# Layer 1's product of u and D moved from ScalarE to VectorE in a four-layer megakernel

## The chip, the cores and the metric

The kernel runs on one core of one Trainium2 chip. The metric is the device time of one execution in microseconds (us), of which the median of several runs is given; less is better. TensorE (PE), VectorE (DVE), ScalarE (ACT), GpSimd (POOL) and SyncE (SP, which issues DMAs) each run a program of their own, strictly in order, and wait for one another by semaphores.

## What is computed

Sixteen sequences (B = 16) of 256 tokens and 256 channels pass through four layers: two state-space layers (layer 0 with two scans in opposite directions, layer 1 a Mamba block), then two attention layers. All is float32. The part that matters here is in layer 1:

```python
xm = silu(conv(x @ W_in))                 # u: 256 tokens x 512 channels
dt = softplus(dtr @ W_dt + b_dt)
def step(hst, inp):                       # 16 states per channel
    hst = hst * exp(dt_t * A) + (dt_t * x_t) * B_t
    y = einsum('bds,bs->bd', hst, C_t)
y = ys + xm * D_param                     # "u times D"
y = y * silu(z)
```

So u is used twice: in the product of dt and u, which feeds the scan, and in u times D, which is added to the scan's output y. D holds one number per channel.

## The kernel before, in words

**Units and ticks.** All three state-space scans (s = 0 and 1 of layer 0, s = 2 of layer 1) are cut into units of one state and one half of the channels (256 channels on 128 partitions as two blocks, times 256 tokens: tiles of 128x512). There are 96 units per sequence (64 of layer 0 for sequence i, 32 of layer 1 for sequence i-1), 1,536 in all. A unit costs: `dbut`, two products of dt*u with B (one by ACT, L788, one by POOL, L798); four transposes by PE into `ps_b` (L710); `decay`, two exponentials by ACT (L777); the scan by DVE (L818, `hst`); `g`, the product with C by POOL (L833); and four transposes by PE that add g up in `ps_v` (L738). A unit u's scan waits for its transposed dbut and its decay; buffers are two to four units deep. PE transposes unit t+2 ahead of the work of tick t and adds up unit t-2 after it; ACT makes decays two units ahead.

**What lies between the units.** Everything else (norms, projections, the preparation of a scan, attention) is cut into pieces by Python generators, each `yield` a seam. Tables written by hand (`PLACES` for the usual sequence, `SPECIAL` for i = -1, 0, 1, 14 to 18) give for each stage and engine the tick at which each piece is put into that engine's program, behind that tick's unit work. Two pieces with the same tick stand in the order of the list `STAGES`. Nothing is decided at run time.

**The stage that the change touches** is `prep2`, the preparation of layer 1's scan, run once per sequence in the middle of layer 0's units of the next one:

- ACT (`prep_scalar`, L984): copies of projections, exp and log for delta (L1014, L1017); then, after DVE's product of delta and u, u times D in place, four instructions of 128x256 (L1022, each with D's column as the scale), with one seam behind the second; then two copies `dut` (L1029) of the transposed product, each after four transposes by PE (L978).
- DVE (`prep_vector`, L1031): two corrections of delta (L1037), the product delta*u into `du` (L1049, in the trace `pT`, since it shares that buffer; for the last sequence `dut`), a small memset of delta (L1051).
- PE (`prep_tensor`, L940): projections (L946, L968), transposes of `du` (L978); its last piece waits for both `dut` copies.

The semaphore `ud_done_2` tells that u times D is there. Only PE waits for it, when it begins to sum layer 1's first unit of that sequence and adds u in by transposes (L719); in the usual sequence that is at tick 66, whereas u times D has its place at tick 44.

**Around it, in the usual sequence** (ticks from the sequence's start): at tick 44 ACT has a table load and the silu of layer 2's tail (L874, `xt_x`), then both pieces of u times D, then the first `dut`; at tick 45 the second `dut`, which is preceded by another table load (L868, for the decays' exponential). PE at tick 44 has the output projection of layer 2 (L923, L927, which wait for `xt_x`) and the second set of transposes of du, and at tick 46 the first projection of `prep0` (L946) behind the wait for the second `dut`. DVE has the first half of layer 0's gating (L1221, `yg`) at tick 45 and at tick 46 the residual of layer 2 (L1594, which waits for PE's L927) with two rounds of norm statistics (L879, L882); from tick 48 on the scaling of the normed rows (L903, `yv`, `xn_l`). PE then transposes those (L910).

Of the kernel before, what the change touches and what calls it, by code (L numbers as in the profile page):

```python
# [10 lines left out]
ALU = mybir.AluOpType  # L11
ACT = mybir.ActivationFunctionType
# [5 lines left out]
TB, DB, EB = T // P, D // P, E // P  # L18
# [29 lines left out]
               dp0=EB, dp1=EB, dp2=EB, alog0=EB * N, alog1=EB * N, alog2=EB * N,  # L48
# [22 lines left out]
def offsets(widths):  # L71
    at, out = 0, {}
    for name, w in widths.items():
# [66 lines left out]
    },  # L140
    "prep2": {
        "PE": (30.875, 34, 35, 36, 39, 43, 44, 46),
        "ACT": (34, 36, 36.125, 39, 41, 41, 44, 44, 44, 45),
        "DVE": (40, 42, 43),
        "SP": (50, 120),
    },
    "l2a": {
# [120 lines left out]
        },  # L268
        "prep2": {
            "PE": (33, 33, 35, 36, 37, 41, 43, 44),  # L270
            "ACT": (33, 34, 36, 36, 36.667, 37, 41, 41, 41, 43),
            "DVE": (38, 39, 40),
            "SP": (35, 37),
        },
        "ada": {
# [41 lines left out]
        },  # L317
        "prep2": {
            "PE": (28, 31, 32, 34, 38, 43, 45, 46),
            "ACT": (32, 32, 37, 37, 40, 41, 44, 44, 44, 45),  # L320
            "DVE": (38, 42, 44),
            "SP": (46, 128),
        },
        "l2a": {
# [45 lines left out]
        },  # L370
        "prep2": {
            "PE": (21, 21, 22, 24, 28, 29.2, 29.8, 33.875),
            "ACT": (22, 23, 26, 26, 28.5, 28.75, 31.2, 31.4, 31.8, 32.4),
            "DVE": (27.25, 28.5, 29),
            "SP": (23, 25),
        },
        "l2a": {
# [41 lines left out]
        },  # L419
        "prep2": {  # L420
            "PE": (-10.444, -10.333, -10, -9.667, -7, -3, -1, -1),
            "ACT": (-7, -7, -6.5, -6.25, -4, -4, -1, -1, -1, -1),
            "DVE": (-7, -4, -3),
            "SP": (-9, -9),
        },
        "l2a": {
# [85 lines left out]
def build(nc, dram, out):  # L512
    with ExitStack() as ctx:
        def sb(name, shape, dt=F32):
            return ctx.enter_context(nc.sbuf_tensor(name, shape, dt))
# [4 lines left out]
        S = {n: ctx.enter_context(nc.semaphore(n)) for n in SEMS}  # L520
# [14 lines left out]
        c = {k: CO[:, o:o + n] for k, (o, n) in COFF.items()}  # L535
# [24 lines left out]
        def bank(ps_, k, m=None):  # L560
            return ps_[:, k, :] if m is None else ps_[:, k, :].rearrange("p (a n) -> p a n", a=m)
# [18 lines left out]
        u_s = [sb(f"u{s}", [P, EB, T]) for s in range(3)]  # L580
# [19 lines left out]
        def nth(sem, b, value):  # L600

            return b * EACH.get(sem, 1) + value

        def slot(b, s):

            if s == 0 and b == 0:
                return 2
            return 0 if s == 2 and b == LAST - 1 else s

        def du_of(b, s):  # L610

            if s == 2 and b == LAST - 1:
                return dut[1][:, :, :].rearrange("p t (h n) -> p (t h) n", n=T)
            return du
# [9 lines left out]
        def after(eng, b, sem, value):  # L624

            if 0 <= b < LAST:
                eng.wait_ge(S[sem], nth(sem, b, value))
# [237 lines left out]
        def logexp():  # L865

            if table[0] != TABLES:
                nc.scalar.preload_act_table_set(TABLES)  # L868
                table[0] = TABLES
# [114 lines left out]
        def prep_scalar(act, b, s, v, at):  # L984
            bk, i = bank(ps_v, v), slot(b, s)
            ch = act_chain[0]
            yield next(at)
            act.wait_ge(S[f"dbc_full_{s}"], nth(f"dbc_full_{s}", b, 1))
            if s == 0:
                after(act, b - 1, "dt_full_1", 2)  # L990
                after(act, b - 1, "c_stored_1", 16)
            if s == 2 and b < LAST - 1:
                after(act, b - 3, "y3_full", 1)
            elif s == 2:
                after(act, b, "dt_full_1", 2)
                after(act, b, "c_stored_1", 16)
            if s == 1 and b >= 1:
                after(act, b, "dt_full_0", 2)
                after(act, b, "c_stored_0", 16)
            if s == 2 and b == 0:  # L1000
                after(act, b, "dt_full_0", 2)
                after(act, b, "c_stored_0", 16)
            nc.scalar.activation(dbc[i][:, :], bk[0:DBC, 0:T], ACT.Identity,
                                 bias=dbcb[:, s:s + 1]).then_inc(S[f"dbc_sb_{s}"], 1)
            yield next(at)
            act.wait_ge(S[f"bt_full_{s}"], nth(f"bt_full_{s}", b, 1))
            nc.scalar.activation(bcm[i][:, :, :], bk[:, 0:TB * P].rearrange("p (t q) -> p t q", t=TB)[:, :, BROW:DBC],
                                 ACT.Copy).then_inc(S[f"bcm_sb_{s}"], 1)
            for k in range(2):
                yield next(at)  # L1010
                act.wait_ge(S[f"dt_full_{s}"], nth(f"dt_full_{s}", b, k + 1))
                d = delta[i][:, 2 * k:2 * k + 2, :]
                logexp()
                ch.done(nc.scalar.activation(d, bank(ps_v, v, 2), ACT.Exp))  # L1014
                yield next(at)
                logexp()
                nc.scalar.activation(d, d, ACT.Ln, bias=1.0).then_inc(S[f"sp_log_{s}"], 1)  # L1017
            yield next(at)
            act.wait_ge(S[f"du_ready_{s}"], nth(f"du_ready_{s}", b, 1))
            dp = (c["dp0"], c["dp1"], c["dp2"])[s]  # L1020
            for eb in range(EB):
                last = nc.scalar.activation(u_s[i][:, eb, :], u_s[i][:, eb, :], ACT.Copy, scale=dp[:, eb:eb + 1])  # L1022
                if eb == 1:
                    yield next(at)
            last.then_inc(S[f"ud_done_{s}"], 1)
            for t in range(TB):
                yield next(at)
                act.wait_ge(S[f"dut_full_{s}"], nth(f"dut_full_{s}", b, t + 1))
                nc.scalar.activation(dut[i][:, t, :], bk, ACT.Copy).then_inc(S[f"dut_sb_{s}"], 1)  # L1029

        def prep_vector(dve, ch, b, s, v, edge, at):  # L1031
            i, du = slot(b, s), du_of(b, s)
            for k in range(2):
                yield next(at)
                dve.wait_ge(S[f"sp_log_{s}"], nth(f"sp_log_{s}", b, k + 1))
                d = delta[i][:, 2 * k:2 * k + 2, :]
                nc.vector.scalar_tensor_tensor(out=d, in0=d, scalar=LN_TOP, in1=bank(ps_v, v, 2), op0=ALU.min,  # L1037
                                               op1=ALU.max).then_inc(S[f"dt_read_{s}"], 1)
            yield next(at)
            dve.wait_ge(S[f"dt_read_{s}"], nth(f"dt_read_{s}", b, 2))  # L1040
            if s == 2:
                after(dve, b + 1, "dut_full_1", 2)
                if b < LAST - 1:
                    after(dve, b - 2, "o_full_2", H2 // 2)
            elif s == 0:
                after(dve, b - 2, "dut_full_2", 2)
            else:
                after(dve, b, "dut_full_0", 2)
            nc.vector.tensor_tensor(du, delta[i][:, :, :], u_s[i][:, :, :], ALU.mult).then_inc(S[f"du_ready_{s}"], 1)  # L1049
            dve.wait_ge(S[f"du_ready_{s}"], nth(f"du_ready_{s}", b, 1))  # L1050
            ch.done(nc.vector.memset(delta[i][:, :, edge:edge + 1], RESET))  # L1051
            nc.vector.engine_nop().then_inc(S[f"prep_done_{s}"], 1)

        def prep_sync(sp, b, scans, s, at):
            yield next(at)
            sp.wait_ge(S[f"dbc_sb_{s}"], nth(f"dbc_sb_{s}", b, 1))
            scans.wait_c(sp)
            sp.dma_start(c_rows[slot(b, s)], dbc[slot(b, s)][CROW:CROW + N, :]).then_inc(S[f"c_stored_{s}"], 16)
            yield next(at)
            sp.wait_ge(S[f"c_stored_{s}"], nth(f"c_stored_{s}", b, 16))  # L1060
# [688 lines left out]
        with ExitStack() as pro:  # L1749
            stage_sems, S = S, {**dict(zip(FIRST, S.values())), **{k: S[k] for k in CARRIED}}  # L1750
# [270 lines left out]
        S = stage_sems  # L2021
# [54 lines left out]
        last = [(LAST - 1, s, hh) for s, hh in LAYER1]  # L2076
# [181 lines left out]
```

## Time and profile before

| | us |
|---|---|
| median of 3 runs | 3290.21 (3288.32 to 3298.6) |
| the profiled execution | 3297.11 |
| its span in the profile | 3295.4 |
| lies around the span | 1.7 |

| engine | busy us | share | instructions |
|---|---|---|---|
| PE | 3022.8 | 92% | 21772 |
| DVE | 2678.8 | 81% | 3433 |
| ACT | 2818.3 | 86% | 6502 |
| POOL | 2655.1 | 81% | 3086 |

The profile comes from one execution. "Busy" is the time in which at least one instruction of the engine runs; instructions overlap at their ends by some 0.1 us, so a row that merges two of 0.50 us shows 0.90. In a row, `out<-in` are the program's buffer names, `x4` is the number of instructions merged, and a bracket at the end gives the idle time of the engine before the row and what ended it. The granted TensorE clock has a mean of 0.98 of full speed.

### The profile page before, as it was taken

The page shows a single profiled execution, that of the slowest core. Times are in us where ns is not written, and L with a number is a line of the kernel's source. Part 1 is how long each engine was busy: PE and PEld are TensorE (multiplying, and loading weights), DVE is VectorE, ACT ScalarE, POOL GpSimd, SP SyncE. Part 2 cuts the span into 40 slices and gives each one's busy share as a digit, 9 for nine tenths or more (in the row PEclk, how much of TensorE's full clock was granted, in tenths as well). Part 3 has the DMA queues.
Part 4 walks back from the last instruction along what each step waited for, and adds up shares of the span by engine and source line. Part 5 has one row for each costly group of instructions (what it writes and reads, how often), then busy time and mean ns, then how long its engine had stood idle before and what let it go on. Part 6 is the DMA issues. An engine that isn't in the chain of part 4 may idle for free.

```text
span 3295.4 us, 63649 instructions
## 1 busy us (share of the span) xinstructions
PE 3022.8 (92%) x21772; PEld 2525.4 (77%) x21772; DVE 2678.8 (81%) x3433; ACT 2818.3 (86%) x6502; POOL 2655.1 (81%) x3086
## 2 busy tenths in 40 slices
PE   6778789999999999999999999999999999988896
PEld 3667677778787888888788887878788887876764
DVE  1667788979798988979898998979798997968762
ACT  2768878899999999999999999998999989887843
POOL 0787999889898898988898898989898897868730
PEclk8899999999999999999999999999999999999998
DMA  5121222222222222222222221222222222212100
GB/s 201 55 76 53 73 79 72 78 67 83 69 81 73 71 84 65 85 67 84 67 81 73 68 86 65 85 67 85 67 74 81 68 82 60 72 52 68 57 25 9
DMA packets 133872, 239.57 MB, mean 73 GB/s; under 512 B 15374, under 2 KB 31054, under 8 KB 133296
## 3 DMA queue, kind: packets, MB, share of 16 engines
q1 hardware_dynamic: 133552, 235.50, 23.3%
q8 instruction: 177, 2.90, 0.4%
q14 instruction: 143, 1.17, 0.1%
HBM read 230.36 MB, written 5.08 MB: 71 GB/s over the span
## 4 chain that ended last, share of the span: by engine, by line
PE 55%; ACT 21%; DVE 10%; POOL 7%; issue 5%; DVEq 0%; POOLq 0%; ACTq 0%
PE ps_b L710 12%; PE ps_v L738 12%; ACT decay L777 8%; DVE hst L818 5%; POOL g L833 5%; PE ps_v L917 5%; ACT dbut L788 4%; PE ps_x L923 3%; PE ps_x L1449 3%; PE ps_x L1476 3%; PE ps_v L968 3%; PE ps_v L923 2%; PE ps_x L917 2%; POOL dbut L798 2%; ACT L874 2%
## 5 line engine op out<-in xcount | busy, mean ns | idle before, releaser
L833 POOL TENSOR_TENSOR g<-hst,c_bc 128x512 f32<-128x512 f32 x1536 | 1975.6, 1286 | 428.4 <-PE ps_v L738 394.1
L818 DVE TENSOR_TENSOR_SCAN hst<-decay,ps_b 128x512 f32<-128x512 f32 x1536 | 1821.5, 1209 | 317.1 <-PE ps_b L710 170.6
L777 ACT ACTIVATE decay<-delta,acoef 128x256 f32<-128x256 f32 x3072 | 1379.2, 499 | 26.8 <-DVE hst L818 25.9
L710 PE MATMUL ps_b<-ident,dbut 128*128 128x128 f32 x6144 | 943.0, 277 | 150.2 <-DVE hst L818 65.9
L738 PE MATMUL ps_v<-ident,g 128*128 128x128 f32 x6144 | 941.7, 276 | 13.9 <-ACT u L1130 12.1
L710 PEld LDWEIGHTS ps_b<-ident,dbut 128*128 128x128 f32 x6144 | 706.9, 142 | 231.1 <-issue 138.8
L738 PEld LDWEIGHTS ps_v<-ident,g 128*128 128x128 f32 x6144 | 727.5, 142 | 143.9 <-issue 67.8
L798 POOL TENSOR_SCALAR dbut<-dut,bcm 128x256 f32<-128x256 f32 x1536 | 750.2, 489 | 79.9 <-ACT dut L1029 79.9
L788 ACT ACTIVATE dbut<-dut,bcm 128x256 f32<-128x256 f32 x1536 | 767.9, 501 | 31.5 <-PE ps_b L710 28.9
L1561 DVE TENSOR_REDUCE mxt<-ps_x 128x4 f32<-128x1024 f32 x120 | 144.6, 1205 | 10.1 <-PE ps_x L1449 10.1
L1532 ACT ACTIVATE pT<-ps_x 128x1024 f32<-128x1024 f32 x120 | 121.8, 1015 | 30.3 <-PE ps_x L1487 25.7
L1476 PE MATMUL ps_x<-qT,kT 32*128 32x256 f32 x960 | 135.9, 400 | 4.8 <-ACT pT L1532 4.5
L1449 PE MATMUL ps_x<-kT,qT 32*128 32x256 f32 x960 | 137.8, 404 | 0.0
L923 PE MATMUL ps_v<-weights,yg 128*128 128x256 f32 x512 | 128.1, 385 | 0.0
L917 PE MATMUL ps_v<-xt_a,weights 128*128 128x256 f32 x512 | 126.8, 382 | 0.1
L765 ACT ACTIVATE yt<-ps_v 128x512 f32<-128x512 f32 x64 | 38.0, 594 | 91.6 <-PE ps_v L738 91.6
L923 PE MATMUL ps_x<-weights,xt_l 128*128 128x256 f32 x384 | 106.7, 403 | 5.6 <-DVE kmax L1714 1.8
L1476 PEld LDWEIGHTS ps_x<-qT,kT 32*128 32x128 f32 x960 | 82.0, 184 | 34.9 <-issue 20.4
L1449 PEld LDWEIGHTS ps_x<-kT,qT 32*128 32x128 f32 x960 | 82.9, 186 | 26.1 <-issue 18.3
L923 PEld LDWEIGHTS ps_v<-weights,yg 128*128 128x128 f32 x512 | 91.1, 192 | 12.7 <-DVE yg L1221 2.6
L917 PEld LDWEIGHTS ps_v<-xt_a,weights 128*128 128x128 f32 x512 | 91.2, 192 | 10.0 <-DVE yg L1257 0.8
L1022 ACT ACTIVATE u<-u,columns 128x256 f32<-128x256 f32 x192 | 84.1, 499 | 6.8 <-DVE pT L1049 5.1
(264 smaller groups left out, 3614.9 us busy)
## 6 DMA issues: line engine op xcount, KB each, us to landing
c_bc<-c_rows SPq DMA_DIRECT2D x768, 256.0 KB, 3.1
weights<-in_weights_dram SPq DMA_DIRECT2D x1, 4320.0 KB, 24.3
x<-in_x_dram SPq DMA_DIRECT2D x16, 256.0 KB, 4.0
rows_bc<-mod_rows SPq DMA_DIRECT2D x16, 256.0 KB, 3.9
gate<-mod_rows SPq DMA_DIRECT2D x32, 128.0 KB, 3.6
out_dram<-x SPq DMA_DIRECT2D x16, 256.0 KB, 3.5
wc<-in_wc_dram SPq DMA_DIRECT2D x1, 2048.0 KB, 11.2
maskrow<-mask_rows SPq DMA_DIRECT2D x16, 128.0 KB, 3.3
```

Of the source, the lines that this page charges most:

```text
L710: last = nc.tensor.matmul(ps_b[:, u % 2, e * T + t * P:e * T + (t + 1) * P], dbut[:, u % NDBU, t, e * P:(e + 1) * P], ident[:, :], is_tran ...
L738: last = nc.tensor.matmul(ps_y[:, t, e * P:(e + 1) * P], g[:, u % NG, e, t * P:(t + 1) * P], ident[:, :], is_transpose=True, start=False, ...
L777: last = nc.scalar.activation(decay[:, u % (DA_AHEAD + 2), e, :], delta[slot(b, s)][:, eb, :], ACT.Exp, scale=acoef[:, s, eb, n:n + 1])
L788: nc.scalar.activation(dbut[:, u % NDBU, 0, :], dut[k][:, 0, hh * HALF * P:(hh + 1) * HALF * P], ACT.Copy, scale=bcm[k][:, 0, n:n + 1]).th ...
L798: nc.gpsimd.tensor_scalar(dbut[:, u % NDBU, 1, :], dut[k][:, 1, hh * HALF * P:(hh + 1) * HALF * P], bcm[k][:, 1, n:n + 1], 1.0, ALU.mult, ...
L818: nc.vector.tensor_tensor_scan(line(hst[:, u % NHST, :, :].rearrange("p e t -> p (e t)")), line(decay[:, u % (DA_AHEAD + 2), :, :].rearran ...
L833: nc.gpsimd.tensor_tensor(g[:, u % NG, :, :], hst[:, u % NHST, :, :], c_bc[:, k % NCB * CHUNK + n % CHUNK, :].unsqueeze(1) .broadcast_to([ ...
L917: last = nc.tensor.matmul(dst, weight[:, k, m0:m0 + m], rhs[:, k, :], start=(k == 0), stop=(k == kb - 1))
L923: last = nc.tensor.matmul(dst, lhs[:, k, t * P:(t + 1) * P], weight[:, k, :], start=(k == 0), stop=(k == kb - 1))
L1449: last = nc.tensor.matmul(bank(pair, j, TB)[:, q, :], a.q[r:r + LANE, hb, q * P:(q + 1) * P], a.k[r:r + LANE, hb, :], start=True, stop=True)
L1476: last = nc.tensor.matmul(bank(pair, j % 2, 2)[:, j // 2, :], a.k[r:r + LANE, hb, m * P:(m + 1) * P], a.q[r:r + LANE, hb, :], start=True, ...
L1561: nc.vector.tensor_reduce(by_head[:, 2 * g_:2 * g_ + 2, :, KEY_AT[g_ // 2 % 2] + 1], a.pairs[g_ % len(a.pairs)][:, 0:2, :].rearrange("p j ...
```

## The change

For s = 2 alone, the four ACT instructions of u times D are left out. DVE makes them instead, as `tensor_scalar` with a multiply by D's column, in two pieces of two instructions, placed one and two ticks behind its product of delta and u (in the usual sequence ticks 44 and 45). `ud_done_2` is now incremented by DVE. All other places stay as they were: ACT's list loses the two entries of u times D, DVE's gains two. At equal ticks `prep2` stands before `l0_post` in `STAGES`, so that the second piece comes before `yg` at tick 45.

```diff
@@ PLACES (usual sequence)
     "prep2": {
         "PE": (30.875, 34, 35, 36, 39, 43, 44, 46),
-        "ACT": (34, 36, 36.125, 39, 41, 41, 44, 44, 44, 45),
-        "DVE": (40, 42, 43),
+        "ACT": (34, 36, 36.125, 39, 41, 41, 44, 45),
+        "DVE": (40, 42, 43, 44, 45),
@@ SPECIAL, i = 1
-            "ACT": (33, 34, 36, 36, 36.667, 37, 41, 41, 41, 43),
-            "DVE": (38, 39, 40),
+            "ACT": (33, 34, 36, 36, 36.667, 37, 41, 43),
+            "DVE": (38, 39, 40, 41, 42),
@@ i = 14
-            "ACT": (32, 32, 37, 37, 40, 41, 44, 44, 44, 45),
-            "DVE": (38, 42, 44),
+            "ACT": (32, 32, 37, 37, 40, 41, 44, 45),
+            "DVE": (38, 42, 44, 45, 46),
@@ i = 15
-            "ACT": (22, 23, 26, 26, 28.5, 28.75, 31.2, 31.4, 31.8, 32.4),
-            "DVE": (27.25, 28.5, 29),
+            "ACT": (22, 23, 26, 26, 28.5, 28.75, 31.8, 32.4),
+            "DVE": (27.25, 28.5, 29, 30, 31),
@@ i = 16
-            "ACT": (-7, -7, -6.5, -6.25, -4, -4, -1, -1, -1, -1),
-            "DVE": (-7, -4, -3),
+            "ACT": (-7, -7, -6.5, -6.25, -4, -4, -1, -1),
+            "DVE": (-7, -4, -3, -2, -1),
@@ prep_scalar
-            yield next(at)
-            act.wait_ge(S[f"du_ready_{s}"], nth(f"du_ready_{s}", b, 1))
-            dp = (c["dp0"], c["dp1"], c["dp2"])[s]
-            for eb in range(EB):
-                last = nc.scalar.activation(u_s[i][:, eb, :], u_s[i][:, eb, :], ACT.Copy, scale=dp[:, eb:eb + 1])
-                if eb == 1:
-                    yield next(at)
-            last.then_inc(S[f"ud_done_{s}"], 1)
+            if s < 2:
+                yield next(at)
+                act.wait_ge(S[f"du_ready_{s}"], nth(f"du_ready_{s}", b, 1))
+                dp = (c["dp0"], c["dp1"])[s]
+                for eb in range(EB):
+                    last = nc.scalar.activation(u_s[i][:, eb, :], u_s[i][:, eb, :], ACT.Copy, scale=dp[:, eb:eb + 1])
+                    if eb == 1:
+                        yield next(at)
+                last.then_inc(S[f"ud_done_{s}"], 1)
@@ prep_vector
             nc.vector.engine_nop().then_inc(S[f"prep_done_{s}"], 1)
+            if s == 2:
+                for pair in range(2):
+                    yield next(at)
+                    for eb in (2 * pair, 2 * pair + 1):
+                        last = nc.vector.tensor_scalar(u_s[i][:, eb, :], u_s[i][:, eb, :], c["dp2"][:, eb:eb + 1], None,
+                                                       ALU.mult)
+                last.then_inc(S["ud_done_2"], 1)
```

## Rows read from the trace of the kernel before

**Rows 1.** The page, busy time and share of the span of each engine.

```profile
PE 3022.8 (92%) x21772; PEld 2525.4 (77%) x21772; DVE 2678.8 (81%) x3433; ACT 2818.3 (86%) x6502; POOL 2655.1 (81%) x3086
```

**Rows 2.** ACT's groups of instructions: busy us, mean ns | idle before, releaser.

```profile
L1022 ACT ACTIVATE u<-u,columns 128x256 f32<-128x256 f32 x192 | 84.1, 499 | 6.8 <-DVE pT L1049 5.1 <-DVE dut L1049 1.7
```

**Rows 3.** The chain of waits, 1629 to 1643 us: start, us, what.

```profile
1632.69 1.59 ACT u L1022 x4
```

**Rows 4.** ACT in order of time, 1627 to 1641 us.

```profile
1630.37 1.28 ACT L874 ACT_TABLE_LOAD   x1
1631.67 1.02 ACT L874 ACTIVATE xt_x<-ps_x,mod_cols 128x256 f32<-128x256 f32 x2
1632.58 1.70 ACT L1022 ACTIVATE u<-u,columns 128x256 f32<-128x256 f32 x4
...
1637.28 0.58 ACT L1029 ACTIVATE dut<-ps_v 128x512 f32<-128x512 f32 x1
```

**Rows 5.** PE in order of time, 1630 to 1643 us.

```profile
1632.74 1.13 PE L923 MATMUL ps_x<-weights,xt_x 128*128 128x256 f32 x4 [0.61 <-ACT xt_x L874]
...
1637.91 1.12 PE L946 MATMUL ps_v<-xt_b,dbcw 128*112 128x256 f32 x4 [0.55 <-ACT dut L1029]
...
1639.36 0.63 PE L710 MATMUL ps_b<-ident,dbut 128*128 128x128 f32 x4
...
1641.59 0.66 PE L910 MATMUL ps_x<-ident,yv 128*128 128x128 f32 x4 [0.30 <-DVE yv L903]
```

**Rows 6.** DVE in order of time, 1628 to 1642 us.

```profile
1630.14 2.33 DVE L818 TENSOR_TENSOR_SCAN hst<-decay,ps_b 128x512 f32<-128x512 f32 x2
...
1632.97 1.21 DVE L818 TENSOR_TENSOR_SCAN hst<-decay,ps_b 128x512 f32<-128x512 f32 x1
1635.21 0.69 DVE L1594 TENSOR_TENSOR x<-ps_x,x 128x512 f32<-128x512 f32 x1 [1.03 <-PE ps_x L927]
...
1638.02 2.34 DVE L818 TENSOR_TENSOR_SCAN hst<-decay,ps_b 128x512 f32<-128x512 f32 x2
1640.28 1.26 DVE L903 TENSOR_SCALAR yv<-x,mv,nrm 128x256 f32<-128x256 f32 x2
```

**Rows 7.** DVE's L1594 in the first and the last of 11 equal sequences.

```profile
698.77 0.69 DVE L1594 TENSOR_TENSOR x<-ps_x,x 128x512 f32<-128x512 f32 x1 [1.03 <-PE ps_x L927]
...
2570.80 0.69 DVE L1594 TENSOR_TENSOR x<-ps_x,x 128x512 f32<-128x512 f32 x1 [1.03 <-PE ps_x L927]
```

**Rows 8.** Busy us (and instructions) of PE, PEld, DVE, ACT, POOL; clock, DMA.

```profile
1641.50:1672.50 31.00, 30.89 (x220) 27.39 (x221) 27.66 (x32) 29.94 (x75) 28.19 (x33) 1.00 0.23 72
```

**Rows 9.** DVE's nearest instructions by their line: ns min/median/max, first and last start.

```profile
L1999 DVE TENSOR_SCALAR gather<-itok,token x2: 346/350/353, 47.1 to 47.3; 128x256 f32<-128x256 f32 x2
...
L903 DVE TENSOR_SCALAR yv<-yv,mv,nrm x2: 391/398/406, 1628.0 to 1628.3; 128x256 f32<-128x256 f32 x2
...
L903 DVE TENSOR_SCALAR xn_a<-x,mv,nrm x2: 1446/1936/2425, 1550.6 to 1552.9; 128x256 f32<-128x256 f32 x2
```

**Rows 10.** POOL in order of time, 1628 to 1643 us.

```profile
1630.98 0.48 POOL L798 TENSOR_SCALAR dbut<-dut,bcm 128x256 f32<-128x256 f32 x1
1631.63 1.27 POOL L833 TENSOR_TENSOR g<-hst,c_bc 128x512 f32<-128x512 f32 x1 [0.16 <-PE ps_v L738]
1632.87 0.48 POOL L798 TENSOR_SCALAR dbut<-dut,bcm 128x256 f32<-128x256 f32 x1
1636.20 1.27 POOL L833 TENSOR_TENSOR g<-hst,c_bc 128x512 f32<-128x512 f32 x1 [2.85 <-PE ps_v L738]
```

**Rows 11.** PE in sequence i = 2, and DVE near the end of the steady part.

```profile
509.57 0.65 PE L978 MATMUL ps_v<-ident,pT 128*128 128x128 f32 x4 [1.62 <-ACT dut L1029]
...
3095.85 0.61 DVE L1728 SCALAR_TENSOR_TENSOR shared<-ps_x,kmax,blockmask 128x128 f32<-128x128 f32 x2 [0.51 <-PE ps_x L1652]
```

## The prediction

> **What bounds the kernel now.** I read the page first: PE is busy for 92% of the span, the others for 81 to 86% [rows 1]. That says PE leads on average, not that it leads where the change is. So next I took ACT's groups: u times D is 192 instructions and 84.1 us of ACT [rows 2]; a third of it, 64 instructions of layer 1, moves. 84.1 / 3 = 28 us of ACT's busy time go. Then the chain of waits in one usual sequence: it does contain the four instructions, 1.59 us of them [rows 3]. Taken literally that promises 1.6 us per sequence. The rest of this prediction is about why I don't take it.
>
> Next came the engines in order of time over the same stretch. The reader is to follow two strands that both begin with ACT's silu `xt_x`, which stands ahead of u times D.
>
> Strand one (ACT): table load from 1630.37, silu to 1632.69, u times D from 1632.58 for 1.70, and at its end the second `dut` at 1637.28 [rows 4]. PE waits 0.55 us for that `dut` and starts L946 at 1637.91 [rows 5].
>
> Strand two (PE and DVE): PE starts layer 2's output projection at 1632.74, as soon as the silu is there [rows 5]; DVE's residual L1594 waits for its end and starts at 1635.21, after 1.03 us idle; behind it come the norm statistics, and only at 1638.02 the next scans [rows 6]. PE's transposes for the scan two units on start at 1639.36, and they need the scan that began at 1638.02 and, by the row's mean, took 1.2 us [rows 5, 6]. DVE goes on without a break to `yv` at 1640.28, and PE waits 0.30 us for that at 1641.59 [rows 5, 6]. From there PE is full: 30.89 of 31.00 us [rows 8].
>
> So both strands end at PE, and strand two ends last: when PE has been let go early at 1637.91, it stops again at 1639.36 for the scan. Nothing of strand two passes through u times D. And what moves PE's start at 1641.59 moves the whole sequence, for in the 31 us behind it there is no idle time in which to catch up [rows 8]. DVE's idle 1.03 us before L1594 is all the slack that strand two has; it is the same in the first and the last of 11 sequences (i = 3 to 13) [rows 7].
>
> **The change part by part.**
>
> *ACT loses four instructions per sequence.* 1.70 us of ACT go [rows 4], 1.6 of them net. The first `dut` comes 1.6 us earlier, but PE reaches the transposes behind it only after the projection, so nobody gains. The second `dut` comes about 1.5 us earlier and PE's 0.55 us at 1637.91 vanish [rows 5]. PE does its L946 and one sum of states, and then waits for the scan at 1639.36 as it did. Gain at the end of the stretch: 0. What hides the gain is DVE's work from 1635.21 to 1639.2; if that were gone, up to 1.6 us per sequence would show.
>
> *DVE gains four instructions per sequence,* two behind the scan that starts at 1630.14 and two behind the next, before `yg` and before the scan of 1632.97 [rows 6]. All four lie ahead of L1594. The trace has none of this form from DVE. The nearest rows: `gather`, also 128x256 from SBUF to SBUF with one column as scalar, 350 ns, two of them starting 0.2 to 0.3 us apart; `yv<-yv`, with two columns, about 400 ns, starts 0.3 apart, both pairs while POOL does nothing long [rows 9]. That is the lower bound, 0.3 us each. The upper one is `xn_a`, of the same shape as the latter: 1.45 and 2.43 us in one sequence [rows 9], with nothing different but what POOL is doing; 1.9 us each. Between them stands `yv<-x` at 1640.28, 1.26 us for two, 0.63 each [rows 6]. A gain from the added work is excluded, since nothing waits for it before tick 66.
>
> Which it is follows from POOL's rows. A pair that meets a POOL instruction is longer by about what is left of it. The first pair would start at about 1631.3: POOL's `dbut` ends at 1631.46, its next `g` starts at 1631.63 [rows 10]; the pair fits between if it is let in first: 0.6 us. This puts the scan and the second pair to about 1633.0: `g` ends at 1632.90 or a little later and a `dbut` of 0.48 stands behind it, after which POOL is idle until 1636.20 [rows 10]. So the second pair costs 0.6 plus a piece of a dbut: 0.75 us. Sum 1.35 us, against 4 x 0.3 = 1.2 as the lower end. The upper end, with `g` (1.27) let in before the second instruction and a whole dbut before the third and the fourth, is 1.2 + 1.27 + 2 x 0.48 = 3.4 us. I take 1.35 because the stretch is nearer to `gather` and `yv<-yv`: POOL is idle for 2.85 us of it.
>
> Per sequence: 1.35 - 1.03 = 0.32 us later. `yg` and the scan of 1632.97 are late by up to 1.35 too, but PE asks for them only after 1636 (it is in the projection from 1632.74 on), so that is covered.
>
> Here the Trainium skill speaks against the change. Its page "SBUF — State Buffer", section "Who interferes with whom", says that VectorE and GpSimd share one pair of ports, which a `tensor_scalar` in a two-port mode holds alone for the whole instruction, whoever comes second waiting in full. The 1.45 and 2.43 us of `xn_a` beside the 0.35 of `gather` agree. By that rule alone, with a wait at each of the four, the sum would be the upper end, 3.4 us.
>
> *The other five sequences.* i = 1: ACT waits for PE before `dut` anyway and DVE idles soon after; 0. i = 2: PE waits 1.62 us for the first `dut` [rows 11], the one place where u times D is plainly in the way; but the scans behind it come later by the 1.35, so of 1.6 gained I count 0 and keep -1 to +0.5 for the range. i = 14 and 15: DVE idles for microseconds there; 0. i = 16: the first pair comes before L1728, which has 0.51 us idle before it [rows 11], in a stretch where POOL has two `g` back to back; +0.5, at most +1.5.
>
> *The sum.* 11 x 0.32 + 0.5 = 3.5 + 0.5 = 4.0 us. The profiled execution took 3297.1, so 3301.1 of its kind; that execution lies 6.9 above the median of the three runs, and the sum is a difference, so I put it on the median: 3290.2 + 4.0 = 3294. No DMA is issued or moved and no queue of SP or POOL is passed. DVE has no new wait.
>
> **The rivals.**
>
> 1. *POOL wins the race (slower).* In the first pair, the second instruction asks at about 1631.6, when `g` at 1631.63 is just about to start [rows 10]. If `g` comes first, the pair costs 0.6 + 1.3 and the second then meets an idle POOL: 0.6. That is 2.5 us, 2.5 - 1.03 = 1.5 us per sequence, 11 x 1.5 + 0.5 = 17, giving 3307. If it only half meets it, 1.0 per sequence, 3302. It decides from 0.85 us per sequence on ((9.9 - 0.5) / 11, the 9.9 being the 0.3% below). For it: `xn_a` [rows 9], and that all 11 sequences are alike, so that a lost race is lost 11 times. Against: `g` waits for PE until 1631.6, after the pair has begun. Chance 0.26. (The Trainium skill, "SBUF — State Buffer", "Who interferes with whom", says that the first to start keeps the pair of ports; it does not say who is first here.)
> 2. *The chain of waits is right (faster).* ACT's strand is the longer one: then 1.6 us per sequence less, in 13 sequences 20.8 us, or, cut by DVE's 0.32, 1.3 x 11 = 14: 3270 to 3276. For it: the chain [rows 3], and ACT shows no idle time from 1629 to 1641. Against: DVE's rows, which are as unbroken and hold L1594, whose releaser is PE. Chance 0.09.
> 3. *All is covered (no change).* The pairs cost 1.2 or less and the two ends cancel; 3290. It differs from my forecast in a size that can't be measured and shares its chance, 0.65 together.
>
> **How the numbers follow.** A measurement of this kernel tells some 0.3% from no change, 9.9 us here (the three runs lie 10 us apart). Forecast and rival 3 (3287 to 3298): within, 0.65. Rival 1: mostly slower, a little of it still within; I give 0.24 to slower and 0.02 to within. Rival 2: 0.09 to faster. That makes 0.09, 0.67 and 0.24. The range is to leave out 0.2: 0.09 for rival 2 and the rest above the upper end. Low end: no cost and a gain of 1 at i = 2, less what runs scatter, 3285. High end: rival 1 at 1.5 per sequence and +1.5 at i = 16, 3290.2 + 16.5 + 1.5 = 3308.
>
> **What would show it.** In the changed profile: the ACT group u<-u has 128 instructions and the new DVE group 64, with a mean of 350 to 450 ns if I am right, above 700 if rival 1 is. DVE's idle time before L1594 falls from 1.03 to about 0, and L1594 is late. PE's 0.55 us before L946 is gone, and PE stands instead at the L710 after it, released by DVE's scan. The distance between two sequences grows from 187.2 us ((2570.80 - 698.77) / 10, [rows 7]) by 0.3. If it shrinks by more than 0.9, my reading of strand two is wrong; if the new instructions cost over 0.6 us each, the price is.

## The result, and the profile after

The changed kernel took 3300.78 us (median of 9 runs, 3295.16 to 3305.24) against 3290.21 of the kernel before (9 runs beside it): a ratio of 1.0029, 95% interval 1.0019 to 1.0038. That is 6 to 13 us slower, about 10, just at the 0.3% that were named as the bound of what can be told. A second set of the same kernel gave 3299.38 and 1.0026 (1.0013 to 1.0039). The forecast was 3294.0, range 3285 to 3308. So the range held the time, but 10 is not 4, and the steps have to be looked at one by one. The profiled execution after took 3303.45 us, its span 3301.7. Medians and ratios, here and below, leave out one slow execution in each of two variants (14402 and 3872 us).

The page after, busy time and share of each engine, to be read against [rows 1]:

```profile
PE 3022.4 (92%) x21772; PEld 2526.3 (77%) x21772; DVE 2705.4 (82%) x3497; ACT 2794.5 (85%) x6438; POOL 2658.8 (81%) x3086
```

DVE has 64 instructions more and ACT 64 fewer. ACT's busy time falls by 23.8 us (28 had been put down), DVE's grows by 26.6. PE's busy time is the same to 0.4 us, so what the change costs is, by this profile, idle time of PE. By the new code's lines (ns: minimum, median, maximum; then the first and the last start), the moved work:

```profile
L1058 DVE TENSOR_SCALAR u<-u,columns x64: 321/336/1401, 319.3 to 3106.9; 128x256 f32<-128x256 f32 x64
```

Median 336 ns, but a maximum of 1401: most of the 64 went undisturbed, some did not. Which ones matters. First the usual sequence, the counterpart of [rows 6]; DVE in order of time:

```profile
1633.96 0.59 DVE L1058 TENSOR_SCALAR u<-u,columns 128x256 f32<-128x256 f32 x2
1634.46 1.21 DVE L818 TENSOR_TENSOR_SCAN hst<-decay,ps_b 128x512 f32<-128x512 f32 x1
1635.60 0.59 DVE L1058 TENSOR_SCALAR u<-u,columns 128x256 f32<-128x256 f32 x2
1636.10 0.68 DVE L1229 TENSOR_TENSOR yg<-ps_v,act_x 128x512 f32<-128x512 f32 x1
1636.70 1.21 DVE L818 TENSOR_TENSOR_SCAN hst<-decay,ps_b 128x512 f32<-128x512 f32 x1
1637.89 0.69 DVE L1602 TENSOR_TENSOR x<-ps_x,x 128x512 f32<-128x512 f32 x1
...
1640.70 2.30 DVE L818 TENSOR_TENSOR_SCAN hst<-decay,ps_b 128x512 f32<-128x512 f32 x2
1642.92 1.28 DVE L903 TENSOR_SCALAR yv<-x,mv,nrm 128x256 f32<-128x256 f32 x2
```

Each pair puts off what stands behind it by 0.50 us (1633.96 to 1634.46; 1635.60 to 1636.10), 1.0 in sum. The residual, L1594 before and L1602 now, had 1.03 us of idle time before it [rows 6] and now has no bracket. From it to `yv` there are 5.03 us, before 5.07. The slack was used up almost exactly, and nothing was carried on. PE over the same stretch, the counterpart of [rows 5]:

```profile
1635.42 1.13 PE L923 MATMUL ps_x<-weights,xt_x 128*128 128x256 f32 x4 [0.60 <-ACT xt_x L874]
...
1639.87 1.03 PE L946 MATMUL ps_v<-xt_b,dbcw 128*112 128x256 f32 x4
...
1642.04 0.63 PE L710 MATMUL ps_b<-ident,dbut 128*128 128x128 f32 x4 [0.70 <-DVE hst L818]
...
1644.25 0.66 PE L910 MATMUL ps_x<-ident,yv 128*128 128x128 f32 x4 [0.28 <-DVE yv L903]
```

The 0.55 us before L946 are gone, and 0.70 us before the next L710 have appeared, released by DVE's scan: a wait for ACT was exchanged for a wait for DVE. From the projection's start to the transposes of `yv` it is 8.83 us now, 8.85 before (1632.74 to 1641.59). And over ten sequences DVE's rows, to be read against [rows 7]:

```profile
701.32 0.69 DVE L1602 TENSOR_TENSOR x<-ps_x,x 128x512 f32<-128x512 f32 x1
...
2573.05 0.69 DVE L1602 TENSOR_TENSOR x<-ps_x,x 128x512 f32<-128x512 f32 x1
```

(2573.05 - 701.32) / 10 = 187.17 us per sequence; before 187.20. **The 11 usual sequences cost nothing.** So the 6 to 13 us lie outside them. At i = 1 one sees the other kind of instruction. DVE:

```profile
319.29 1.60 DVE L1058 TENSOR_SCALAR u<-u,columns 128x256 f32<-128x256 f32 x2
320.82 1.21 DVE L818 TENSOR_TENSOR_SCAN hst<-decay,ps_b 128x512 f32<-128x512 f32 x1
321.95 1.64 DVE L1058 TENSOR_SCALAR u<-u,columns 128x256 f32<-128x256 f32 x2
```

and POOL at the same time:

```profile
319.46 1.28 POOL L833 TENSOR_TENSOR g<-hst,c_bc 128x512 f32<-128x512 f32 x1
...
322.16 1.27 POOL L833 TENSOR_TENSOR g<-hst,c_bc 128x512 f32<-128x512 f32 x1 [0.93 <-DVE hst L818]
```

A pair takes 1.60 and 1.64 us instead of 0.59, and in each pair it is the second instruction (at 319.53 and 322.19) that takes 1.4: it asks 0.07 and 0.03 us after POOL's `g` has started, and is done only 0.15 us after that `g`. The first ones take 0.3. In the usual sequence it is the other way round: the second instruction starts at 1634.21, and `g` at 1634.31. That is rival 1, but not in the eleven sequences in which it was feared: twice in i = 1, and once each in i = 2, 15 and 16 (1362, 1401 and 1355 ns).

### The profile page after: what moved, and what is told of

Read it like the earlier page. It is cut to its first block, busy times and chain, and to the rows that moved or that the text cites. A ratio compares the mean times of both kernels' runs of the same rounds, so it can differ in the third digit from the quotient of the medians.

```text
span 3301.7 us, 63649 instructions
## 1 busy us (share of the span) xinstructions
PE 3022.4 (92%) x21772; PEld 2526.3 (77%) x21772; DVE 2705.4 (82%) x3497; ACT 2794.5 (85%) x6438; POOL 2658.8 (81%) x3086
## 4 chain that ended last, share of the span: by engine, by line
PE 56%; ACT 17%; DVE 14%; POOL 6%; issue 5%; DVEq 0%; POOLq 0%; ACTq 0%
PE ps_b L710 13%; PE ps_v L738 12%; ACT decay L777 6%; DVE hst L818 6%; POOL g L833 5%; PE ps_v L917 4%; ACT dbut L788 3%; PE ps_x L923 3%; PE ps_x L1484 3%; PE ps_x L1457 3%; PE ps_v L968 3%; PE ps_v L923 2%; PE ps_x L917 2%; POOL dbut L798 2%; DVE stats L879 1%
## 5 line engine op out<-in xcount | busy, mean ns | idle before, releaser
L710 PE MATMUL ps_b<-ident,dbut 128*128 128x128 f32 x6144 | 944.9, 277 | 158.3 <-DVE hst L818 77.3
L710 PEld LDWEIGHTS ps_b<-ident,dbut 128*128 128x128 f32 x6144 | 708.5, 143 | 240.3 <-issue 140.7
L1038 DVE SCALAR_TENSOR_TENSOR delta<-delta,ps_v 128x512 f32<-128x512 f32 x96 | 63.7, 663 | 25.9 <-ACT delta L1017 25.8
```

Of the source, the lines that this page charges most:

```text
L710: last = nc.tensor.matmul(ps_b[:, u % 2, e * T + t * P:e * T + (t + 1) * P], dbut[:, u % NDBU, t, e * P:(e + 1) * P], ident[:, :], is_tran ...
```

## The experiments

Three theories stood at the outset. *Two strands*: PE is held by two nearly equal ones, DVE's and ACT's, so freeing ACT gives nothing and DVE's slack of 1.0 us is just used up. *The chain of waits*: u times D stands in PE's way and would give 1.6 us if DVE did not charge for it. *The edges*: the time is lost in the sequences that are not usual. The variants that follow come from the changed kernel, by a set of the sequences in which ScalarE keeps u times D with its old places (and DVE its old three); their lines are shifted by 9, so that the new instructions are L1067, the scan L827, `g` L842, PE's transposes for the scan L719 and the first projection of `prep0` L955.

```diff
+ON_ACT = {...}   # the sequences in which ScalarE keeps u times D
-            if s < 2:
+            if s < 2 or b + 1 in ON_ACT:
...
-            if s == 2:
+            if s == 2 and b + 1 not in ON_ACT:
```

### Where the time lies: the usual sequences or the others

**The usual ones alone** (`ON_ACT = {1, 14, 15, 16}`).

> u times D by VectorE in the 12 sequences with the usual places (i = 2 to 13), by ScalarE in i = 1, 14, 15, 16. Theory A (the first profile of the change: in each of 11 equal sequences PE gains 0.72 us at L946 and loses 0.81 us at the L710 behind it, the distance of two sequences stays 187.05 us; the 10 us come from the edges): within 3 us of the kernel before, the new instructions at 0.25 us a start, DVE's idle time before L1602 zero, distance of sequences 187.05. Theory B (each usual sequence costs 0.8 us or so, and that profile was not typical): 8 to 10 us over the kernel before. Theory C (ScalarE's strand was the longer one): 10 us or more under it.

**The others alone** (`ON_ACT = {2, ..., 13}`).

> u times D by VectorE only in i = 1, 14, 15 and 16, by ScalarE in the 12 usual sequences. Theory A (edges): all of the slowdown is here, 3298 to 3303 us. Theory B (usual sequences): within 3 us of the kernel before. In its profile A expects two of the four instructions at i = 1 and one at i = 15 and 16 to take about 1.4 us (a lost race against POOL), and a product of delta and u near 346 us at over 5 us instead of 1.7.

**The changed kernel again**, beside them.

> The changed kernel once more, for a second profile and more times. If the edges (deterministic orders of POOL and DVE) make the difference, the product near 346 us takes over 5 us again and the shift against the kernel before is +2.6 us from i = 3 on again. If PE's clock makes part of it, the two stretches at half speed near 2681 and 2737 us (4 us together) are at other places or gone; the time stays at 3298 to 3303 either way.

Measured, against 3290.59 of the kernel before in this batch: usual ones alone 3292.17, ratio 1.0000 (0.9987 to 1.0013); others alone 3299.76, 1.0026 (1.0012 to 1.0039); changed kernel 3299.38, 1.0026. So four sequences cost what all 16 cost, and twelve cost nothing that can be told.

The trace of the usual ones alone holds one exception among i = 3 to 13, which the changed kernel's two traces do not have. In i = 8, DVE and POOL:

```profile
1630.66 1.64 DVE L1067 TENSOR_SCALAR u<-u,columns 128x256 f32<-128x256 f32 x2
```

```profile
1630.89 1.27 POOL L842 TENSOR_TENSOR g<-hst,c_bc 128x512 f32<-128x512 f32 x1 [0.41 <-DVE hst L827]
```

The scan ahead of the pair came 0.4 us late, the second instruction asked at 1630.91, 0.02 us behind `g`, and took 1401 ns; PE, compared with the kernel before, comes 1.0 us later behind it than ahead of it. The same happened in the same sequence of the run with all but i = 1 (1397 ns, 1.0 us). So the race of the usual sequences is won narrowly, and a loss there does reach PE.

### What the four instructions are worth to ScalarE and VectorE

**No u times D at all in the usual sequences.** In i = 2 to 13 the product is left out altogether, and what is added to y is u; ScalarE has it in i = 1, 14, 15 and 16.

```diff
-                    for eb in (2 * pair, 2 * pair + 1):
-                        last = nc.vector.tensor_scalar(...)
-                last.then_inc(S["ud_done_2"], 1)
+                nc.vector.engine_nop().then_inc(S["ud_done_2"], 1)
```

> In the 12 usual sequences u times D is left out altogether (u is added to y without D); the other four have it on ScalarE as before. It measures what these four instructions are worth to the time, whichever engine has them. Theory A (PE's strand through DVE's L1594 and its statistics ends last; ScalarE's 1.6 us are covered by it): 0 to 3 us under the kernel before; PE's 0.55 us before L946 gone and PE standing at the next L710 for about the same time. Theory C (the chain of waits is right): 1.3 to 1.6 us per sequence, 15 to 19 us under it, distance of sequences 185.5.

It took 3293.98, ratio 1.0004 (0.9993 to 1.0014). Even with neither engine doing the work, nothing is gained in 12 sequences; at 1.6 each, 19 should have been. PE shows why:

```profile
1632.28 1.03 PE L955 MATMUL ps_v<-xt_b,dbcw 128*112 128x256 f32 x4
...
1634.44 0.63 PE L719 MATMUL ps_b<-ident,dbut 128*128 128x128 f32 x4 [0.70 <-DVE hst L827]
```

The stop of 0.70 us before the transposes is the one of the changed kernel, and DVE's slack before the residual is 1.00 us again. So it is DVE's strand from the residual to the scan that ends last. The chain of waits, which put 1.59 us of u times D on the path [rows 3], is refuted as a price. It was right as a record: a strand that ends 0.1 us later than another is on the path in full.

**A longer DVE strand.** Each of the four instructions in i = 2 to 13 is cut into four of 64 columns; the work is the same and the fixed part is paid 16 times.

```diff
-                        last = nc.vector.tensor_scalar(u_s[i][:, eb, :], ...)
+                        for q in range(0, T, 64):
+                            last = nc.vector.tensor_scalar(u_s[i][:, eb, q:q + 64], ...)
```

> As the run with the usual sequences alone (VectorE in i = 2 to 13), but each of the four instructions cut into four of 64 columns: 16 instead of 4, the same product. The change used up VectorE's idle 1.03 us before the residual exactly. An estimate from the starts 0.25 us apart of the whole ones: 0.16 us a start, so 2.6 us instead of 1.0 per sequence, 1.5 us beyond the slack. Theory E (what moves PE behind the stretch moves the whole sequence, since PE is full for 31 us): distance of sequences 188.5, time 15 to 20 us over the kernel before, more if POOL wins races. Theory F (later slack takes it up): distance 187.05, within 4 us.

It took 3321.34, ratio 1.0090 (1.0075 to 1.0106), with 189.75 us from sequence to sequence, 2.6 more than the 187.17 of the changed kernel. DVE in one of them:

```profile
1641.77 2.52 DVE L1068 TENSOR_SCALAR u<-u,columns 128x64 f32<-128x64 f32 x8
1644.21 1.21 DVE L827 TENSOR_TENSOR_SCAN hst<-decay,ps_b 128x512 f32<-128x512 f32 x1
1645.34 1.36 DVE L1068 TENSOR_SCALAR u<-u,columns 128x64 f32<-128x64 f32 x8
```

Start to start the two groups put off DVE by 2.44 and 1.28 us (1641.77 to 1644.21; 1645.34 to 1646.62, where `yg` starts), 3.7 in sum. The first group is longer by 1.2 us because one of its instructions lost a race and took 1256 ns; so it went in every one of these sequences, which is why 31 us came and not the 15 to 20 of the expectation. Less the slack of 1.03 that is 2.7, and 2.6 came. **What goes beyond the slack is carried over in full,** which is what the prediction said of PE's 31 full microseconds [rows 8].

**A longer ACT strand.** ScalarE has u times D in every sequence, in i = 2 to 13 as eight instructions of 128 columns.

```diff
-                    last = nc.scalar.activation(u_s[i][:, eb, :], ...)
+                    step = 128 if s == 2 and 2 <= b + 1 <= 13 else T
+                    for q in range(0, T, step):
+                        last = nc.scalar.activation(u_s[i][:, eb, q:q + step], ...)
```

> u times D by ScalarE in all 16 sequences as before, but in the 12 usual ones each instruction cut into two of 128 columns: 8 instead of 4, estimated 0.29 us a start instead of 0.40, so 0.75 us more of ScalarE per sequence. In the kernel before PE reached the L710 behind L946 at 1639.30 by its own work and the scan let it start at 1639.36: the two strands were equal within 0.1 us. Theory E (two equal strands, so lengthening ScalarE's costs at once though shortening it gives nothing): distance 187.7, 6 to 10 us over the kernel before. Theory G (ScalarE's strand has slack): within 3 us.

It took 3296.77, ratio 1.0021 (1.0008 to 1.0034). Between 690 and 2560 us of the kernel before, PE's work came 7.5 us later than there, 0.7 per sequence. The other variants stay within 1 us over this stretch (DVE in quarters aside). PE:

```profile
1628.27 0.66 PE L987 MATMUL ps_v<-ident,pT 128*128 128x128 f32 x4 [0.38 <-ACT dut L1042]
...
1631.37 1.12 PE L955 MATMUL ps_v<-xt_b,dbcw 128*112 128x256 f32 x4 [0.70 <-ACT dut L1042]
...
1635.05 0.65 PE L919 MATMUL ps_x<-ident,yv 128*128 128x128 f32 x4 [0.39 <-DVE yv L912]
```

The first two waits are now for ACT. Its eight instructions took 2.34 us from the first start to the next instruction's, against 1.6 for the four, so 0.7 longer, and 0.7 us are lost at once. So ACT's strand had no slack either. In the kernel before, both strands end within 0.1 us of each other: shortening ACT's gives nothing, lengthening it costs at once, and lengthening DVE's costs from 1.03 us on. That shortening DVE's alone would give nothing either follows from this, but no run did it.

### Which of the other sequences

> u times D by VectorE in i = 1 alone, by ScalarE in the 15 other sequences. The edges made 10.9 us together. Theory A1 (i = 1: two of the four instructions lose the race to POOL's g, 1.4 us each, and the units behind them wait, in a stretch where nothing is full): 2 to 5 us over the kernel before. Theory A2 (all of it lies in the last sequences): within 1.5 us of it.

> u times D by VectorE in i = 14 and 15 alone. Two instructions of 0.5 us and one of 1.4 us in the profile of the change; VectorE idles for microseconds around both. Theory A1: 1 to 3 us over the kernel before (scans behind them late by about 1 us each, and yv caught by POOL for 1.4 us at i = 14). Theory A2 (the last sequences make nearly all): 4 us or more.

> u times D by VectorE in i = 16 alone, the last sequence, where the two pairs stand before L1736 and L1741 of layer 3 and before the steady part ends. One instruction of 1.4 us there. Theory A1: 1 to 3 us over the kernel before; theory A2: 4 us or more; my prediction had 0.5, at most 1.5.

> The kernel before once more, for a second profile. The first profile of before has a product of delta and u of 1.68 us at 346.7 us where the changed kernel had 5.3; the kernel with the usual sequences alone, whose programs are the same as before up to there, had 5.3 too. Theory D (that race is chance): 5.3 or 1.7, either is possible, and the time doesn't tell them apart. Time 3288 to 3298, distance of sequences 187.05 us.

The edits are `ON_ACT` without 1, without 14 and 15, without 16. Against 3290.24 of the kernel before in this batch:

| VectorE has u times D in | us | ratio |
|---|---|---|
| i = 1 | 3298.97 | 1.0025 (1.0014 to 1.0036) |
| i = 14, 15 | 3293.84 | 1.0008 (0.9999 to 1.0016) |
| i = 16 | 3289.83 | 1.0002 (0.9992 to 1.0012) |
| none, one execution, for its trace | 3297.38 | |

Most of it is i = 1 alone: some 8 us, where the expectation had 2 to 5. Its DVE rows there, from another execution on another program, show the same pattern as those of the changed kernel:

```profile
324.51 1.61 DVE L1067 TENSOR_SCALAR u<-u,columns 128x256 f32<-128x256 f32 x2
326.04 1.21 DVE L827 TENSOR_TENSOR_SCAN hst<-decay,ps_b 128x512 f32<-128x512 f32 x1
327.17 1.64 DVE L1067 TENSOR_SCALAR u<-u,columns 128x256 f32<-128x256 f32 x2
```

and POOL's:

```profile
324.68 1.29 POOL L842 TENSOR_TENSOR g<-hst,c_bc 128x512 f32<-128x512 f32 x1
...
327.38 1.27 POOL L842 TENSOR_TENSOR g<-hst,c_bc 128x512 f32<-128x512 f32 x1 [0.92 <-DVE hst L827]
```

The second instructions started at 324.76 (1358 ns) and 327.41 (1394 ns), 0.08 and 0.03 us behind a `g`. PE there and some 27 us later:

```profile
330.08 0.63 PE L719 MATMUL ps_b<-ident,dbut 128*128 128x128 f32 x4 [1.04 <-DVE hst L827]
...
334.42 0.63 PE L719 MATMUL ps_b<-ident,dbut 128*128 128x128 f32 x4 [0.16 <-DVE hst L827]
...
356.80 1.11 PE L987 MATMUL ps_v<-ident,pT 128*128 128x128 f32 x4 [3.78 <-DVE pT L1059]
```

The last row is a second find. It waits for the next product of delta and u on DVE (layer 0's of the next sequence). In this execution the product took 5.33 us, and in the kernel before 1.68:

```profile
L1049 DVE TENSOR_TENSOR pT<-delta,u x1: 1680/1680/1680, 346.7 to 346.7; 128x1024 f32<-128x1024 f32 x1
```

The long one occurs without the change too, for instance in the second profile of the kernel before:

```profile
353.46 1.12 PE L978 MATMUL ps_v<-ident,pT 128*128 128x128 f32 x4 [3.78 <-DVE pT L1049]
```

It was long in all four executions with VectorE's instructions at their places of i = 1 (the changed kernel twice, the others alone, i = 1 alone) and in three of nine with ScalarE's. By how much each execution lost between 317 and 360 us against the first profile of before (PE's instructions compared one by one):

| u times D of i = 1, product | later between 317 and 360 us, by execution |
|---|---|
| VectorE, long | 3.8, 2.7, 3.0, 3.8 |
| ScalarE, long | 1.3, 1.2, 1.3 |
| ScalarE, short | 0, -0.4, -1.2, -1.3, -1.3, -1.3 |

So the long product goes with about 2 us and the two lost races with about 2 more. Together VectorE's four (mean 3.3) lie 3.5 us above the mean of ScalarE's nine (-0.2). Part of this is TensorE's clock: the four executions at -1.2 and -1.3 have no stretch at half speed between 317 and 360 us, all the others have 3.4 to 10.2 us of it (the changed kernel's first profile 10.2).

### Is it the place, or the engine?

**Only i = 1, and later.** VectorE has u times D in i = 1 alone, but at ticks 50 and 51, where DVE waits in any case.

```diff
-            "DVE": (38, 39, 40, 41, 42),
+            "DVE": (38, 39, 40, 50, 51),
```

> u times D by VectorE in i = 1 alone, its two pairs at ticks 50 and 51 instead of 41 and 42. At 41 and 42 the second instruction of each pair asked 0.03 and 0.08 us after POOL's g had started and waited for all of it. Theory H (the cost at i = 1 is these two lost races and what they set off): 0 to 4 us over the kernel before if the races are won at the new place, which the instructions' durations tell (0.33 us each, or 1.4). Theory I (it is the removal from ScalarE that changes the phase there): 6 to 9 us as with the old places.

**All but i = 1.** The change everywhere else (`ON_ACT = {1}`).

> The change in all sequences but i = 1, which keeps ScalarE. Theory A (i = 1 makes most of the 10 us, i = 14 to 16 some 2.5): 1 to 4 us over the kernel before. If it is at 8 or more, the effect of i = 1 alone was chance.

The first took 3289.11, ratio 0.9995 (0.9985 to 1.0006); the second 3291.98, ratio 1.0003 (0.9991 to 1.0015). The four instructions of the first:

```profile
L1067 DVE TENSOR_SCALAR u<-u,columns x4: 320/569/585, 331.8 to 334.2; 128x256 f32<-128x256 f32 x4
```

At ticks 50 and 51 no instruction waits for a whole `g` (the maximum is 585 ns), the product behind them took 1.54 us, and the cost is gone. Two ways of undoing one place undo most of the slowdown. Neither beats the kernel before, whose time lies within both intervals; a version that does beat it did not come out of this, and from the run without u times D none is to be had from moving these instructions in the usual sequences.

## Why the prediction was right, and where not

- **Two strands, the second ends last: right.** PE's 0.55 us vanished, and it stood at the L710 instead, released by the scan, as forecast. The run without u times D shows the same stop.
- **What moves PE at 1641.59 moves the sequence: right.** 2.7 us beyond the slack gave 2.6.
- **The price on DVE, 1.35 us per sequence: too high.** It measured 1.0: all four ran undisturbed at 0.25 us start to start. The step "the second pair costs 0.6 plus a piece of a dbut: 0.75 us" failed, as did the lower end, 4 x 0.3 = 1.2. (The upper end, 3.4, holds three waits and not the four that the prediction names beside it.) With 1.0 against a slack of 1.03, the term 11 x 0.32 = 3.5 was 0. The row that could have told was there: `gather`, "two of them starting 0.2 to 0.3 us apart". I took 0.3 from it, near its duration, where what counts for a queue is the distance of starts.
- **i = 1: the step that failed.** "ACT waits for PE before `dut` anyway and DVE idles soon after; 0." I asked whether idle time stood behind the instructions, and not whom they meet. It measured 8 us by its own run (1.0014 to 1.0036 of 3290: 5 to 12). Two of four instructions lost a race, 1.36 and 1.39 us. Each pair then puts off the scan behind it by 1.5 us where I had reckoned 0.6, in a part where PE waits for DVE's scans.
- **i = 14, 15: 0 forecast.** Its run says +2.6 us by the ratio, with an interval that touches no change; one instruction of the eight, in i = 15, lost a race (1402 ns), and in its trace PE falls behind by 1.1 us between 2750 and 2800, in i = 14, as in all four others that have the change there. Where ScalarE has the work it stays within 0.1 in six traces; the DVE quarters gain 0.3, and i = 1 alone, where a stretch at half speed fell away, 1.6. The rest is not settled. **i = 16: +0.5 forecast.** The traces show 0.8 to 1.2 between 3095 and 3130, against at most 0.2 with ScalarE, and one lost race of 1355 ns; the time can't tell it from 0. **i = 2: 0 forecast,** and nothing there that tells it from chance, though one race was lost in three of the four traces with the change there.
- **Rival 1** had the mechanism right and the price near, with the wrong place. It put 1.3 us on a lost race and 1.5 us on a sequence that has one; a pair with a lost race puts off the scan behind it by 1.5 instead of 0.5, and the two usual sequences that had one cost 1.0. Its "all 11 sequences are alike, so that a lost race is lost 11 times" held for the race that is won, save for i = 8 in two of the four traces. **Rival 2,** the chain of waits, is refuted by the run without u times D. **Rival 3** is what the usual sequences did.

So the net result landed in the range partly by luck, through two terms missed in opposite directions: 3.5 too much in the usual sequences, and 8 too little at i = 1.

Three things stay open.

- *The rest of i = 1.* The traces account for 3.5 us at i = 1, where the run's ratio gives 8 and its interval begins at 5; single executions differ from each other by up to 8 us before 300 us and by several at the end, so that one profile can't show the rest. The granted clock that every execution notes points at a part of it: its mean is 0.9793 to 0.9801 in the four sets with VectorE at the places of i = 1, 0.9812 to 0.9816 in the kernel before, and 0.9806 to 0.9826 in the other variants (the DVE quarters apart, 0.9787). The difference, some 0.0018 of 3290 us, makes an estimated 6 us at most, and among the kernel before's executions a long one is low in clock and a short one high (3296.93 us at 0.979, 3281.84 at 0.985). Whether the lower clock costs this time, or only follows from PE's longer waits, no run decides.
- *Two stretches at half speed.* In the changed kernel's profile 4.8 us are added between 2600 and 2750, where PE shows two stretches at half speed (near 2680 and 2736) that the kernel before does not have; the usual ones alone and i = 16 alone have them too (4.3 and 4.8 us), and its own second profile has not (1.8): that is not the change's, but what brings them is open.
- *The long product.* Whether it follows from the four instructions, or is only made likelier, is argued from 4 of 4 against 3 of 9, not shown; with the four at ticks 50 and 51 it was short, in one execution.

## What to carry to other kernels

Before moving an instruction to VectorE, list for each place where it will stand what GpSimd starts within 0.1 us of it, and do this in the unusual sequences first: a usual one that wins its race costs nothing 11 times, and a single badly placed one cost 0.25% of the kernel. A race won by 0.1 us turns when the work ahead of it is 0.4 us late, as in i = 8. A wait on the chain of waits is worth only its distance to the next strand, here 0; look for the instruction behind it on every other engine before counting it. Count short VectorE instructions in a row by the distance of their starts, and compare the sum with the idle time before the next instruction that waits for another engine.

## What the runs showed of the hardware

- **A race is decided by hundredths of a microsecond, and the loser waits for the whole instruction.** VectorE's 128x256 `tensor_scalar` with one column took 0.33 to 0.35 us when it started 0.10 us ahead of POOL's `g`, and 1.35 to 1.40 when it started 0.02 to 0.10 behind. The 128x64 ones narrow it: 0.24 us for one that started 0.02 us ahead, 1.32 and 1.33 for two that started less than 0.01 us ahead. This agrees with the Trainium skill, "SBUF — State Buffer", "Who interferes with whom", by which whoever issues first holds the shared ports for the whole instruction. It was as repeatable as the schedule: lost in both pairs of i = 1 in four executions of three programs, and won in i = 3 to 13 in both executions of the changed kernel, while two other programs lost it once, in i = 8.
- **Two of them in a row cost 0.50 us, not 0.67:** the second starts 0.25 us behind the first. Four times as many of 64 columns took 221 ns at least and 1.28 us for eight, 0.16 us start to start: a quarter of the columns for 0.64 of the time.
- **A `tensor_tensor` with both inputs in SBUF can stand for several of POOL's instructions.** The product of delta and u has a median of 1.22 us over 47 and a maximum of 4.9 in the kernel before; near 346 us it took 1.7 in one execution of that kernel and 5.3 in another, at the same place of the schedule:

```profile
346.72 1.68 DVE L1049 TENSOR_TENSOR pT<-delta,u 128x1024 f32<-128x1024 f32 x1
```

```profile
348.07 5.33 DVE L1049 TENSOR_TENSOR pT<-delta,u 128x1024 f32<-128x1024 f32 x1
```

  Both times it started some 0.85 us behind a `g`. In the short one POOL's next `dbut` took 1.55 us instead of 0.48, so it was POOL that waited; in the long one POOL ran `dbut`, `g`, `dbut`, `g` and `dbut` at their usual lengths ahead of it. The Trainium skill, "SBUF — State Buffer", "Who interferes with whom", says that such an instruction contends with POOL's reads. What decides who is served, no run here shows.
